# A four-layer post-norm transformer on one core: the second and the last feed-forward block as one stage each for both batches

## The reference

```python
# layer 1 (counted from 0), ternary weights; INTER = 1376
gate = jnp.einsum('bsh,ih->bsi', x, Wg) * ag
up = jnp.einsum('bsh,ih->bsi', x, Wu) * au
h = jax.nn.silu(gate) * up
out = jnp.einsum('bsi,hi->bsh', h, Wd) * ad
# layer 3; each weight is a narrow matrix repeated four times, plus a rank-2 term
w = jnp.tile(wq, (1, 4))
base = x @ w.T
lora = x @ A.T @ B.T
y = base + lora * 0.5            # used for w1, w3 and w2
out = y2(silu(y1(x)) * y3(x))    # w1q, w3q: (1376, 128); w2q: (512, 344)
```

## Time and profile before

| | us |
|---|---|
| median of three runs | 2150.57 (2146.85 to 2151.94) |
| the profiled execution, its time | 2150.87 |
| the profiled execution, span from first to last instruction | 2148.8 |
| PE busy in the span | 1981.9 (92%) |
| DVE, ACT, POOL busy | 1102.5, 773.3, 742.0 |
| Ffn1, both batches, from the first to the next stage's first matmul | 1193.67 to 1425.52 |
| Ffn3, both batches, to the end of the span | 2015.31 to 2148.8 |

### The profile page before, as it was taken

One profiled execution on the slowest core, in us unless ns is written; L12 is line 12 of the kernel. 1 busy time (PEld: TensorE's weight loads), 2 busy tenths in 40 slices (PEclk: granted clock), 3 DMA queues, 4 the chain that ended last, 5 costly groups with the idle time before them and its releaser, 6 DMA issues.

```text
span 2148.8 us, 28198 instructions
## 1 busy us (share of the span) xinstructions
PE 1981.9 (92%) x10552; PEld 1252.8 (58%) x10552; DVE 1102.5 (51%) x1979; ACT 773.3 (36%) x1643; POOL 742.0 (35%) x1199
## 2 busy tenths in 40 slices
PE   5999978999999999999998897969999898999887
PEld 3454435777777777777776685844444454544333
DVE  4676465555555555555554415135556355655444
ACT  1565423333333333333332322312555313565301
POOL 2454315434333333434331433412444212443100
PEclk9899979999999999999999897989999999999889
DMA  7323000101010010101000521134333006212000
GB/s 192 44 34 103 1 20 0 50 1 50 3 48 30 21 50 1 50 1 50 1 30 0 196 88 59 44 43 49 58 61 104 15 1 75 46 32 71 10 20 20
DMA packets 45336, 95.01 MB, mean 44 GB/s; under 512 B 7593, under 2 KB 35625, under 8 KB 41897
## 3 DMA queue, kind: packets, MB, share of 16 engines
q1 hardware_dynamic: 42610, 90.86, 16.6%
q10 hardware_dynamic: 2592, 2.36, 0.8%
HBM read 62.20 MB, written 2.10 MB: 30 GB/s over the span
## 4 chain that ended last, share of the span: by engine, by line
PE 82%; DVE 10%; issue 3%; ACT 2%; DMA 2%; POOL 1%; POOLq 0%; ACTq 0%; SPq 0%; DVEq 0%
PE PS L1361 10%; PE PS L1430 8%; PE PS L1413 6%; PE PS L1386 6%; PE PS L1754 6%; PE PS L544 5%; PE PS L441 5%; PE PS L522 5%; PE PS L488 4%; PE PS L569 3%; PE PS L1398 3%; PE PS L1372 3%; PE PS L1765 3%; PE PS L1730 3%; PE PS L456 2%
## 5 line engine op out<-in xcount | busy, mean ns | idle before, releaser
L962 ACT ACTIVATE PB<-PS 128x512 f32<-128x512 f32 x480 | 281.0, 599 | 240.8 <-PE PS L522 237.9
L738 DVE TENSOR_REDUCE NM<-PS 128x2 f32<-128x1024 f32 x192 | 209.2, 1091 | 182.9 <-PE PS L490 181.9
L867 POOL TENSOR_SCALAR_AFFINE_SELECT PB<-PB 128x256 f32<-128x256 f32 (+1 forms) x480 | 174.3, 367 | 322.6 <-ACT PB L962 316.5
L1559 ACT COPY PRT<-PS 128x512 f32<-128x512 f32 (+3 forms) x256 | 108.6, 425 | 415.5 <-PE PS L1398 409.9
L488 PE MATMUL PS<-KQ 96*128 96x512 bf16 (+3 forms) x768 | 188.5, 310 | 30.7 <-DMA KQ<-LOW 16.3
L1519 DVE TENSOR_REDUCE NX<-PS 128x1 f32<-128x512 f32 (+3 forms) x256 | 124.2, 490 | 169.7 <-PE PS L1387 167.8
L1667 POOL TENSOR_SCALAR PR<-PR,RCP 128x512 f32<-128x512 f32 (+3 forms) x256 | 135.7, 535 | 199.8 <-DVE RCP L1507 193.4
L522 PE MATMUL PS<-KQ 99*128 99x512 bf16 (+3 forms) x768 | 183.8, 305 | 5.6 <-DMA KQ<-NMT 2.5
L1386 PE MATMUL PS<-kT,qT 128*128 128x512 f32 (+3 forms) x512 | 183.5, 440 | 4.3 <-ACT PR L1614 4.1
L441 PE MATMUL PS<-XTT,WA 128*128 128x512 f32 x288 | 149.0, 627 | 13.2 <-DVE ident_masks_b L2166 11.8
L1614 ACT ACTIVATE PR<-PS,NX 128x512 f32<-128x512 f32 (+3 forms) x256 | 136.3, 532 | 47.6 <-DVE NX L1519 46.3
(11 more groups left out here) (258 smaller groups left out, 3991.0 us busy)
## 6 DMA issues: line engine op xcount, KB each, us to landing
KQ<-HI SPq DMA_DIRECT2D x90, 128.0 KB, 3.9
KQ<-MID SPq DMA_DIRECT2D x72, 128.0 KB, 4.6
WB<-f_w SPq DMA_DIRECT2D x12, 768.0 KB, 4.4
WB<-w1o SPq DMA_DIRECT2D x8, 1024.0 KB, 8.1
WC<-f_w SPq DMA_DIRECT2D x10, 768.0 KB, 4.5
WB<-w1a SPq DMA_DIRECT2D x8, 768.0 KB, 4.3
WB<-w1b SPq DMA_DIRECT2D x8, 768.0 KB, 5.9
WA<-w SPq DMA_DIRECT2D x6, 1024.0 KB, 7.4
```

What stands on the lines that cost most here:

```text
L738: x = dve.tensor_reduce(nm[:, h:h + 2, i], PS[:, b:b + 2, 0:(i + 1) * P], AX.X, ALU.max, negate=True)
L867: pool.affine_select(blocks, blocks, [[0, count], [1, P]], ALU.is_ge, 0.0, base=0, channel_multiplier=-1).then_inc(s16["probs_ready"].sem, 1)
L962: act.activation(PB[:, n % PBS, :], PS[:, 4 + n % 2, :], ACT.Exp, scale=self.scale)\
```

## The change

`Ffn1` and `Ffn3` become one stage each for both batches, in the manner of `Ffn0` and `Ffn2`. Ffn1 counts its groups through, m = 0 to 21, where m = 11 to 21 are those of the second batch; the split of the second batch's x is made at m = 2 to 5, and the first batch's tail is placed among groups 11 to 13. `H1` and `AD` move into a part of `WB`. Ffn3 makes Z of both batches at its start, the first batch's output tiles after groups 1, 3, 5 and 7 of the second batch and its tail beside them, and SP writes each row tile to `out` as soon as it is finished. The diff, cut to its core (the removed functions are in the listing above; the counts `.at(n)` of a batch become plain numbers everywhere):

```diff
-        H1 = sb("H1", [P, 2, T], F32, F1)
...
-        AD = sb("AD", [P, D], F32, F1)
...
-        XH2 = sb("XH2", [P, NC, T], F32R, F1)
-        XL2 = sb("XL2", [P, NC, T], F32R, F1)
+        XH2 = sb("XH2", [P, NB, NC, T], F32R, F1)
+        XL2 = sb("XL2", [P, NB, NC, T], F32R, F1)
...
+        H1 = WB[:, 3072:4096].rearrange("p (s n) -> p s n", s=2)
+        AD = WB[:, 4096:4608]
...
+            def __init__(self):
+                one = Tail(0, y_done=(f1["down"], M1), mul=AD)
+                self.tails = [one, Tail(1, y_done=(f1["down"], M), mul=AD, after=one)]
...
+            def gate_up(self, pe, m):
+
+                b = m // M1
+                high, low = WH[:, m % RING, :], WL[:, m % RING, :]
+                if m >= 2:
+                    pe.wait_ge(f1["h"].sem, m - 1)
+                pe.wait_ge(f1["w_hi"].sem, m + 1)
...
+            def down(self, pe, m):
+
+                high, low = WH[:, m % RING, 1024:1536], WL[:, m % RING, 1024:1536]
+                pe.wait_ge(f1["h_lo"].sem, m + 1)
+                for t in range(NT):
+                    if m == M1:
+                        pe.wait_ge(self.tails[0].s_t.sem, self.tails[0].s_t.at(t + 1))
...
+                for m in range(M):
+                    self.gate_up(pe, m)
+                    if m == M1 + 1:
+                        for t in range(2):
+                            self.tails[0].turn(pe, t, PS[:, 4 + t, :])
+                    elif m == M1 + 2:
+                        for t in range(2, NT):
+                            self.tails[0].turn(pe, t, PS[:, 4 + t, :])
+                        self.down(pe, M1)
+                        self.down(pe, M1 + 1)
+                    elif m:
+                        self.down(pe, m - 1)
+                self.down(pe, M - 1)
+                self.tails[1].tensor(pe)
...
+                    if m == M1 + 2:
+                        for t in range(2, NT):
+                            self.tails[0].take(act, t, PS[:, 4 + t, :])
...
-                    if m + 2 < M1:
+                    if m + 2 < M:
                         self.high(act, m + 2)
-                self.tail.scalar(act)
+                    if m == M1 + 1:
+                        for t in range(2):
+                            self.tails[0].take(act, t, PS[:, 4 + t, :])
+                self.tails[1].scalar(act)
...
+            def split_x(self, dve, b, c):
+
+                dve.tensor_copy(XH2[:, b, c, :], XTT[:, b, c, :]).then_inc(f1["x_hi"].sem, 1)
+                dve.wait_ge(f1["x_hi"].sem, NC * b + c + 1)
+                dve.tensor_tensor(XL2[:, b, c, :], XTT[:, b, c, :], XH2[:, b, c, :].bitcast(F32), ALU.subtract)\
+                   .then_inc(f1["x_lo"].sem, 1)
...
             def vector(self, dve, st):
                 for c in range(NC):
-                    dve.tensor_copy(XH2[:, c, :], XT[:, c, :]).then_inc(f1["x_hi"].sem, 1)
-                for c in range(NC):
-                    dve.wait_ge(f1["x_hi"].sem, f1["x_hi"].at(c + 1))
-                    dve.tensor_tensor(XL2[:, c, :], XT[:, c, :], XH2[:, c, :].bitcast(F32), ALU.subtract)\
-                       .then_inc(f1["x_lo"].sem, 1)
+                    self.split_x(dve, 0, c)
                 dve.wait_ge(f1["scales_loaded"].sem, 32)
-                for m in range(M1):
-                    dve.wait_ge(f1["silu"].sem, f1["silu"].at(m + 1))
-                    dve.scalar_tensor_tensor(H1[:, m % 2, :], PS[:, 2 + m % 2, :], AGU[:, 1, m:m + 1],
-                                             SG[:, m % 2, :], ALU.mult, ALU.mult).then_inc(f1["h"].sem, 1)
-                    dve.wait_ge(f1["h_hi"].sem, f1["h_hi"].at(m + 1))
-                    dve.tensor_tensor(HL[:, m % 2, :], H1[:, m % 2, :], HH[:, m % 2, :].bitcast(F32),
-                                      ALU.subtract).then_inc(f1["h_lo"].sem, 1)
-                self.tail.vector(dve, st)
+                one = self.tails[0]
+                for m in range(M):
+                    self.hidden(dve, m)
+                    if 2 <= m < 2 + NC:
+                        self.split_x(dve, 1, m - 2)
+                    if m == M1:
+                        one.mean(dve, st, 0, PS[:, 4, :])
+                        one.mean(dve, st, 1, PS[:, 5, :])
+                        one.finish(dve, 0)
+                    if m == M1 + 1:
+                        one.finish(dve, 1)
+                        one.mean(dve, st, 2, PS[:, 6, :])
+                        one.mean(dve, st, 3, PS[:, 7, :])
+                        one.finish(dve, 2)
+                        one.finish(dve, 3)
+                self.tails[1].vector(dve, st)
...
+                for m in range(M):
+                    pool.wait_ge(f1["w_hi"].sem, m + 1)
                     w = f1w[m % RING]
                     pool.tensor_tensor(WL[:, m % RING, :], w, WH[:, m % RING, :].bitcast(F32), ALU.subtract)\
                         .then_inc(f1["w_lo"].sem, 1)
-                self.tail.gpsimd(pool)
+                    if m in (M1 + 2, M1 + 3):
+                        for t in range(2):
+                            self.tails[0].root(pool, 2 * (m - M1 - 2) + t)
+                self.tails[1].gpsimd(pool)
...
+                for m in range(RING, M):
+                    sp.wait_ge(f1["w_lo"].sem, m - RING + 1)
+                    self.load(sp, m)
...
+            def __init__(self):
+                one = Tail(0, self.y_tile, last=True)
+                self.tails = [one, Tail(1, self.y_tile, last=True, after=one)]
+
+            def y_tile(self, pe, b, t):
+                tail = self.tails[b]
+                if t == 0:
+                    pe.wait_ge(f3["z2"].sem, b + 1)
+                    pe.wait_ge(f3["hs"].sem, 3 * (b + 1))
+                if t >= 2:
+                    pe.wait_ge(tail.s_v.sem, tail.s_v.at(t - 1))
...
+            def gate_up(self, pe, b, m):
+                n = M3 * b + m
+                if n >= 2:
+                    pe.wait_ge(f3["h"].sem, n - 1)
...
+            def tensor(self, pe):
+                pe.wait_ge(S_f3.sem, 80)
+                for b in range(NB):
+                    for c in range(NC):
+                        x = pe.matmul(PS[0:LR, 7 - 2 * b, :], f3_a13[:, c, :], XTT[:, b, c, :],
+                                      start=(c == 0), stop=(c == NC - 1))
+                    x.then_inc(f3["z_psum"].sem, 1)
+                pe.wait_ge(f3_b_lo.sem, 2)
+                for b in range(NB):
+                    pe.wait_ge(f3["xs"].sem, b + 1)
+                    pe.wait_ge(f3["z"].sem, b + 1)
+                    for m in range(M3):
+                        self.gate_up(pe, b, m)
+                        if b and m in (1, 3, 5, 7):
+                            self.y_tile(pe, 0, m // 2)
+                    self.two_columns(pe, b)
+                for t in range(NT):
+                    self.y_tile(pe, 1, t)
...
+            def narrow(self, dve, st, b):
+
+                st.done(dve.tensor_tensor(XS[:, b, :], XTT[:, b, 0, :], XTT[:, b, 1, :], ALU.add))
+                st.link(dve.tensor_tensor(XS2[:, :], XTT[:, b, 2, :], XTT[:, b, 3, :], ALU.add))
+                dve.tensor_tensor(XS[:, b, :], XS[:, b, :], XS2[:, :], ALU.add).then_inc(f3["xs"].sem, 1)
+                dve.wait_ge(f3["z_psum"].sem, b + 1)
+                dve.tensor_scalar(Z[:, b, :], PS[0:LR, 7 - 2 * b, :], 0.5, None, ALU.mult).then_inc(f3["z_hi"].sem, 1)
+                dve.wait_ge(f3["z_hi"].sem, b + 1)
                 low = slice(32, 64)
-                dve.scalar_tensor_tensor(Z[low, :], PS[low, 7, :], 0.5, Z[low, :].bitcast(F32),
+                dve.scalar_tensor_tensor(Z[low, b, :], PS[low, 7 - 2 * b, :], 0.5, Z[low, b, :].bitcast(F32),
                                          ALU.mult, ALU.subtract).then_inc(f3["z"].sem, 1)
...
+            def vector(self, dve, st):
+                self.narrow(dve, st, 0)
+                low = slice(64, 96)
+                dve.wait_ge(f3_b_hi.sem, 1)
+                dve.tensor_tensor(BP[low, 0:M3 * P], f3_b[low, 0:M3 * P],
+                                  BP[low, 0:M3 * P].bitcast(F32), ALU.subtract).then_inc(f3_b_lo.sem, 1)
+                one = self.tails[0]
+                for b in range(NB):
+                    for m in range(M3):
+                        n = M3 * b + m
+                        dve.wait_ge(f3["silu"].sem, n + 1)
+                        if n == M3:
+                            dve.wait_ge(f3["z2_psum"].sem, 1)
+                        dve.tensor_tensor(H3[:, m, :], PS[:, 2 + m % 2, :], SG3[:, m % 2, :], ALU.mult)\
+                           .then_inc(f3["h"].sem, 1)
+                        if n == 2:
+                            self.narrow(dve, st, 1)
+                        if b and m in (2, 4, 6, 8):
+                            t = m // 2 - 1
+                            one.mean(dve, st, t, PS[:, 4 + t % 2, :])
+                        if b and m in (4, 6, 8, 10):
+                            one.finish(dve, m // 2 - 2)
+                    self.sums(dve, st, b)
```

(61 more changed lines are left out.)

193 lines of the change are left out of this document (68 added, 125 removed).

## The result

The changed kernel takes **2115.78 us** (median of 4, 2114.98 to 2118.62) against 2151.26 for the kernel before on the same chip; the ratio is 0.984, 95% interval 0.982 to 0.986. The forecast was 2119 in a range of 2112 to 2127. The profiled execution took 2115.63 us with a span of 2113.5, 35.3 less than before, where the prediction had 31.3.

What follows compares the result with a forecast made beforehand. PE holds 82% of the chain ending last, so only its idle time, waits for DVE or lower clock can yield. Ffn1 9.5 plus Ffn3 21.8 make 31.3 us; 2150.6 - 31.3 = 2119 us, range 2112 to 2127.

Steps and rivals of the forecast that it cites:

- What goes in Ffn1, 24.8: Ffn1, first batch's tail and second batch's start: 29.7 us, less one group of 5.45, plus 0.5 for HL, vanish: 24.8 us.
- The handover, 10.4 and 2.6 for the clock: Ffn1, first batch's tail placed among groups: 9.5 or 11.4 us extra, taken as 10.4, plus 2.6 for PE's clock.
- I charge one such recovery, 2.6 us: Ffn1, around the first batch's tail: PE's clock falls once after waits, costing 2.6 us; bounds 0 and 5.
- a wait of 2.4 us for tile 2: Ffn1, after group 13: PE waits 2.4 us for DVE's finish, since the means of tiles 2 and 3 meet POOL's WL.
- the middle of two orders: Ffn1, first add of mean against POOL's WL: 9.5 or 11.4 us extra depending on which begins first; 10.4 taken.
- three waits, 2 to 4 us each, 7 to 9 in all: Ffn1, between groups 11 and 14: the new profile would show PE waiting three times for DVE's finish, at these sizes.
- The start, +2.3: Start of Ffn1: casts 3 and 4 stand behind subtractions that wait for POOL, costing 2.3 us more; bounds 0 and 4.
- Ffn3, 21.8: Ffn3 to the end of the span: 111.7 us instead of 133.5, so 21.8 us less; bounds 17 and 23.
- cheap handover: Ffn1: DVE's adds slip in ahead of POOL and PE stays at 2.4 GHz; about 2113 us, chance 0.15.
- The bare handover: Ffn1: DVE, POOL and ACT wait in a ring, PE sees the whole 14.5 us tail; 2125 us, chance 0.12.
- stalled tiles: Ffn3: each of four output tiles waits 2 us for HS, banks or mean; 2127 us, chance 0.08.
- a clock that stays low: Second batch of Ffn1: PE stays at 1.2 GHz as small waits recur; 2210 us over the whole batch, chance 0.02.

## Why the prediction was right, and where it was not

- **What goes in Ffn1, 24.8:** right. 15.0 is 24.8 - 8.6 (handover) - 1.2 (start).
- **The handover, 10.4 and 2.6 for the clock:** the mechanism was right in its parts (adds of `mean` against `WL`, waits for `finish`, one dip of the clock); how they add up was not. The step that failed is "I charge one such recovery, 2.6 us", put on top of a wait of 2.4 us for tile 2. The dip cost 2.2 us in group 13, and the wait behind it was 0, since both are the same time: 8.6 in all in place of 13.0. With group 13 at full clock the 2.4 us were there (2.24). Of the 4.4 us between the two, 2.4 are this wait. Another 0.9 is luck: I took the middle of two orders, and DVE was first by 0.06 us. The first two waits were 1.55 and 1.84 where I had 2.1 and 2.1 for that very order (0.8), and the dip was 0.4 cheaper. The forecast of "three waits, 2 to 4 us each, 7 to 9 in all" failed: they were 1.55, 1.84 and 0.32 (for tile 3), 3.7 in all.
- **The start, +2.3:** +1.2. A cast and a subtraction stood behind POOL (3.65 and 3.80 us). But the last cast ended 9.96 us after the first began, 0.4 us earlier than the last subtraction did before (10.36), and not 0.4 later as I had it; and the last 8 of the 21 matmuls behind it ran at full clock (1.81 us).
- **Ffn3, 21.8:** 22.1, term by term: to the first group 9.4 (9.5), groups 27.7 with a wait of 1.0 (26.4 and 1.4), rank-2 term 2.7 (2.8), second batch 41.0 (41.1), the rest 27.7 (27.4), store 2.9 (3.1). Most of its durations came from a row of the same work in the earlier trace rows.
- **Rivals:** "cheap handover" gave nearly the measured time, but not by its mechanism: the clock did fall, and POOL held up two of the four adds. The bare handover, stalled tiles and a clock that stays low were not seen; the second batch's stretch from group 14 on (69.67 us) shows 1.00.
- **The rest:** the two stages together gave 37.1 us; 1.4 us before Ffn1 and 0.3 behind it, in code that the change doesn't touch, went the other way. That the forecast of 2119 lies only 3 us off, with its Ffn1 term 5.5 us off, is in part due to them, and luck.

## What to carry to other kernels

When a wait of PE takes its clock down and another engine's chain runs beside it, draw both chains up to the next meeting and take the longer; don't add the price of the clock to the wait. Then cure both or neither. And look at each place where POOL begins a long instruction on SBUF operands: one wait that lets a few short DVE instructions go first turned 9.0 us of them into 2.5 and won 5.7 us at a start of the kernel before and, together with the casts first, 6.9 in the changed one, where that reordering alone won 1.5.
